# A transformer layer on one NeuronCore: the second FFN product as three products of split operands

## The reference

```python
q = query @ wq + query @ Aq @ Bq * 4.0;  k = query @ wk
v = query @ wv + query @ Av @ Bv * 4.0
q, k = apply_rope(split(q)), apply_rope(split(k))
scores = where(causal, -1e9, einsum('bhqd,bhkd->bhqk', q, k) / 4)
attn_out = (softmax(scores) @ v) @ wo
x = layernorm(x + attn_out)
h = butterfly(x @ W_exp + b_exp, up_weights)
h = gelu(h + up_bias)
y = butterfly(h, down_weights) @ W_con + b_con + down_bias
x = layernorm(x + y)
```

## Time and profile before

| | |
|---|---|
| three runs | 1182.09, 1182.82, 1183.34 us; median 1182.82 us |
| the profiled execution | 1180.9 us, of which its span is 1179.2 us |
| share of the span busy | PE 93%, DVE 71%, ACT 57%, POOL 42% |
| mean granted TensorE clock | 0.962 of full (2.4 GHz); 1.00 from 178 us to 1088 us |
| chain that ended last, by engine | PE 76%, DVE 8%, DMA 8%, issue 3%, ACT 2% |

### The profile page before, as it was taken

One profiled execution on the slowest core, in us unless ns is written; L12 is line 12 of the kernel. 1 busy time (PEld: TensorE's weight loads), 2 busy tenths in 40 slices (PEclk: granted clock), 3 DMA queues, 4 the chain that ended last, 5 costly groups with the idle time before them and its releaser, 6 DMA issues.

```text
span 1179.2 us, 27684 instructions
## 1 busy us (share of the span) xinstructions
PE 1091.7 (93%) x8462; PEld 791.5 (67%) x8462; DVE 840.0 (71%) x1951; ACT 674.4 (57%) x1067; POOL 491.4 (42%) x539
## 2 busy tenths in 40 slices
PE   4677699999999999999999999999999999999976
PEld 3454366767677776767677776767677777766665
DVE  6689867686868678686858678686858778676333
ACT  2277557474656657474656657474656658474601
POOL 5342524435363634435363634435353635433301
PEclk9678799999999999999999999999999999999989
DMA  7773553646465564646465564646465564641201
GB/s 267 162 214 88 167 131 102 185 111 195 93 213 127 182 156 132 174 110 197 95 206 127 182 159 134 169 109 203 93 203 127 181 162 138 166 116 49 74 28 36
DMA packets 94983, 169.90 MB, mean 144 GB/s; under 512 B 14872, under 2 KB 36120, under 8 KB 94944
## 3 DMA queue, kind: packets, MB, share of 16 engines
q1 hardware_dynamic: 93888, 166.53, 51.2%
q10 hardware_dynamic: 832, 1.83, 0.4%
q0 software_dynamic: 224, 1.04, 0.2%
HBM read 92.28 MB, written 77.07 MB: 144 GB/s over the span
## 4 chain that ended last, share of the span: by engine, by line
PE 76%; DVE 8%; DMA 8%; issue 3%; ACT 2%; POOL 1%; SPq 1%; DVEq 0%; POOLq 0%; ACTq 0%
PE ps_m L560 27%; PE ps_m L709 17%; PE ps_m L679 10%; PE ps_m L608 7%; PE ps_t L651 6%; PE ps_m L688 4%; DMA m_scr<-m_row 4%; DVE m_raw L905 2%; PE ps_m L637 2%; DMA q_st<-m_scr 2%; ACT pT L781 1%; DVE gact L991 1%; DVE y L991 1%; PE ps_m L671 1%; PE ps_m L694 1%
## 5 line engine op out<-in xcount | busy, mean ns | idle before, releaser
L781 ACT ACTIVATE pT<-ps_t 128x512 f32<-128x512 f32 x640 | 330.9, 602 | 223.1 <-PE ps_t L651 222.8
L905 DVE TENSOR_REDUCE m_raw<-ps_m 128x1 f32<-128x512 f32 (+2 forms) x768 | 338.6, 505 | 67.8 <-PE ps_m L637 62.3
L1046 POOL TENSOR_SCALAR_AFFINE_SELECT pT<-pT 128x512 f32<-128x512 f32 (+1 forms) x320 | 179.1, 562 | 450.3 <-ACT pT L781 447.4
L709 PE MATMUL ps_m<-w,gact 128*128 128x256 f32 x1024 | 231.6, 382 | 1.1 <-ACT gact L851 1.1
L709 PEld LDWEIGHTS ps_m<-w,gact 128*128 128x128 f32 x1024 | 191.9, 190 | 29.6 <-ACT gact L851 1.5
L608 PE MATMUL ps_m<-k_st,q_st 48*128 48x512 f32 (+3 forms) x1024 | 152.5, 354 | 26.3 <-DMA k_st<-qk_scr 15.1
L679 PE MATMUL ps_m<-pT,v_aug 128*32 128x512 f32 (+3 forms) x2048 | 157.9, 450 | 4.4 <-DVE m_raw L905 3.0
L608 PEld LDWEIGHTS ps_m<-k_st,q_st 48*128 48x128 f32 x1024 | 88.3, 189 | 84.6 <-issue 59.7
L651 PE MATMUL ps_t<-q_st,k_st 50*128 50x512 f32 (+3 forms) x1024 | 129.8, 354 | 12.8 <-DMA q_st<-m_scr 8.6
L952 DVE TENSOR_TENSOR y<-ps_m,y 128x256 f32<-128x256 f32 x64 | 27.2, 425 | 145.9 <-PE ps_m L709 145.9
L679 PEld LDWEIGHTS ps_m<-pT,v_aug 128*32 128x32 f32 x2048 | 58.8, 112 | 90.7 <-issue 78.8
(11 more groups left out here) (106 smaller groups left out, 1601.3 us busy)
## 6 DMA issues: line engine op xcount, KB each, us to landing
qk_scr<-rot_hi SPq DMA_DIRECT2D x64, 512.0 KB, 3.7
q_st<-qk_scr SPq DMA_DIRECT2D x128, 192.0 KB, 4.7
k_st<-qk_scr SPq DMA_DIRECT2D x128, 192.0 KB, 5.0
qk_scr<-rot SPq DMA_DIRECT2D x32, 512.0 KB, 4.0
o_scr<-o_raw SPq DMA_DIRECT2D x64, 256.0 KB, 3.0
r_b<-in_xT SPq DMA_DIRECT2D x17, 512.0 KB, 6.4
o_c<-o_scr SPq DMA_DIRECT2D x32, 256.0 KB
r_b<-r_scr SPq DMA_DIRECT2D x32, 256.0 KB
```

The lines of the kernel that those rows point to most:

```text
L709: mm = pe.matmul(pm[:, 0:D], gact[:, k, n * P:(n + 1) * P], w2[:, k, :], start=(k == 0), stop=(k == NHT - 1))
L781: act.activation(pT[:, g % 2, slot, half * T:(half + 1) * T], ps_t[:, ST_BANK[2 * n + r], :], ACT.Exp, scale=SCALE).then_inc(exp_done, 1)
L905: ins = dve.tensor_reduce(m_raw[:, r, u // 2, qt:qt + 1], scores[:, off:off + (qt + 1) * P], AX.X, ALU.max, negate=True)
L1046: pool.affine_select(out=v, in_=v, compare_op=ALU.is_ge, fill=0.0, base=0, pattern=pattern, channel_multiplier=-1).then_inc(mask_done, 1)
```

## The change

The second FFN product is computed as three products. `w2` becomes `w2_hi` and `w2_lo`. The activation is split by two new steps: `HI` (ACT, two copies of 128x1024 for each half) and `LO` (a subtraction of 128x1024 for each quarter: quarters 0 and 1 on POOL, 2 and 3 on DVE). The pieces of W2 move to phases 3, 3, 4 and 6, those of V to phases 2 and 3. To make room, gact and `g_lo` share one buffer, the upper half of the high part lies in the buffer of x1T, `rot_hi` and `rope_in` are half as large (which adds waits to HIGH and moves a wait of DVE's QK step), the fifth slots of pT are one slot, and set-up tables share a buffer.

```diff
         elif p == 2:
             put("VC", i)
             gemm("QK", i + 1, 3)
             put("QKL", i + 1, 0)
-            gemm("W2", i - 2, 0)
+            if not static or i >= 0:
+                gemm("V", i + 1, 0)
         elif p == 3:
...
-            gemm("W2", i - 2, 1)
+            gemm("V", i + 1, 1)
+            put("LO", i - 2, 2)
+            put("LO", i - 2, 3)
+            gemm("W2", i - 2, 0)
             put("RCP", i - 1, 1)
             put("REC", i - 1, 1)
-            gemm("W2", i - 2, 2)
+            gemm("W2", i - 2, 1)
...
         elif p == 4:
             put("QKL", i + 1, 1)
-            gemm("W2", i - 2, 3)
+            gemm("W2", i - 2, 2)
...
         elif p == 6:
-            if not static or i >= 0:
-                gemm("V", i + 1, 0)
-                gemm("V", i + 1, 1)
+            gemm("W2", i - 2, 3)
             gemm("MT", i, 3)
...
         elif p == 1:
             put("XRES", i - 1, 0)
+            put("HI", i - 2, 1)
...
             put("OUT", i - 2)
+            put("HI", i - 1, 0)
+            put("LO", i - 1, 0)
 
     def last(p):
 
-        if p == 2:
+        if p == 0:
+            put("LO", i - 2, 1)
+        elif p == 2:
             put("ON", i - 1, 0)
...
+        def low_parts(eng, b, j):
+
+            half, part = j // 2, slice(2 * (j % 2), 2 * (j % 2) + 2)
+            g = gact[:, 2 * j:2 * j + 2, :]
+            eng.wait_ge(ghi_done, 4 * b + j + 1)
+            eng.tensor_tensor(g_lo[:, 2 * j:2 * j + 2, :], g, g_hi[half][:, part, :].bitcast(FP32), ALU.subtract)\
+               .then_inc(glo_done[half], 1)
...
                     half = int(kind == "W2B")
-                    pe.wait_ge(gelu_done, 2 * b + half + 1)
-                    for k in range(NHT // 2 * half, NHT // 2 * (half + 1)):
-                        mm = pe.matmul(pm[:, 0:D], gact[:, k, n * P:(n + 1) * P], w2[:, k, :],
-                                       start=(k == 0), stop=(k == NHT - 1))
+                    cols, ks = slice(n * P, (n + 1) * P), range(NHT // 2)
+                    if n == 0:
+                        pe.wait_ge(ghi_done, 4 * b + 2 * half + 2)
+                    for k in ks:
+                        for w in (w2_hi, w2_lo):
+                            pe.matmul(pm[:, 0:D], g_hi[half][:, k, cols], w[:, NHT // 2 * half + k, :],
+                                      start=(half == 0 and k == 0 and w is w2_hi), stop=False)
+                    if n == 0:
+                        pe.wait_ge(glo_done[half], 2 * (b + 1))
+                    for k in ks:
+                        mm = pe.matmul(pm[:, 0:D], g_lo[:, NHT // 2 * half + k, cols],
+                                       w2_hi[:, NHT // 2 * half + k, :],
+                                       start=False, stop=(half == 1 and k == NHT // 2 - 1))
...
+                    if not (isinstance(b, int) and b == 0):
+                        act.wait_ge(qkh_out, 2 * DMA * (2 * b + n))
+                        act.wait_ge(low_done, 2 * b + n)
+                    act.activation(high_of(b, n), rot[:, n, :, :], ACT.Copy).then_inc(high_done, 1)
...
-                    act.activation(w2[:, n, :], pm[:, 0:D], ACT.Copy).then_inc(evac["DM"], 1)
+                    act.activation(w2_hi[:, n, :], pm[:, 0:D], ACT.Copy).then_inc(w2h_done, 1)
...
+                elif kind == "HI":
+
+                    act.wait_ge(gelu_done, 2 * b + n + 1)
+                    wait(act, done["W2"], NT * b)
+                    for j in range(2):
+                        k = NHT // 2 * n + 2 * j
+                        act.activation(g_hi[n][:, 2 * j:2 * j + 2, :], gact[:, k:k + 2, :], ACT.Copy)\
+                           .then_inc(ghi_done, 1)
...
+                elif kind == "DM":
+                    dve.wait_ge(w2h_done, n + 1)
+                    dve.tensor_tensor(w2_lo[:, n, :], pm[:, 0:D], w2_hi[:, n, :].bitcast(FP32),
+                                      ALU.subtract).then_inc(evac["DM"], 1)
+                elif kind == "LO" and n > 1:
+                    low_parts(dve, b, n)
```

More of the change, by code:

```diff
@@ L262, in layer @@
         cs = sb("cs", [P, 2, T])
-        rope_in = sb("rope_in", [P, 4, T])
+        rope_in = sb("rope_in", [P, 2, T])
         rot = sb("rot", [P, 2, 2, T])
-        rot_hi = sb("rot_hi", [P, 2, 2, T], F32R)
+        rot_hi = sb("rot_hi", [P, 2, T], F32R)
         v_new = sb("v_new", [P, NT, D])
@@ L270, in layer @@
         r_b = sb("r_b", [P, 2, T])
-        s_m = sb("s_m", [64, 64])
-        r_m = sb("r_m", [64, 64])
+        small = sb("small", [P, P])
+        s_m, r_m, m_row = small[64:P, 0:64], small[64:P, 64:P], small[0:NM * GH * NT, :]
         x_res = sb("x_res", [P, NT, D])
-        x1T_hi = sb("x1T_hi", [P, KD, T], F32R)
-        x1T_lo = sb("x1T_lo", [P, KD, T], F32R)
-        gact = sb("gact", [P, NHT, T])
+        x1T = sb("x1T", [P, 2, KD, T], F32R)
+        with ExitStack() as before_g_hi0:
+            setup = before_g_hi0.enter_context(nc.sbuf_tensor("setup", [P, P + 32], FP32))
+        g_hi0 = sb("g_hi0", [P, NHT // 2, T], F32R)
+        with ExitStack() as before_g_lo:
+            gact = before_g_lo.enter_context(nc.sbuf_tensor("gact", [P, NHT, T], FP32))
+        g_lo = sb("g_lo", [P, NHT, T], F32R)
         y = sb("y", [P, NT, D])
@@ L351, in layer @@
         rope_done, high_done, low_done = sem("rope_done"), sem("rot_hi_done"), sem("rot_lo_done")
-        qk_out, ones = sem("qk_out"), sem("ones")
+        qkh_out, qkl_out, ones = sem("qk_hi_out"), sem("qk_lo_out"), sem("ones")
         fill = [sem(f"fill{g}") for g in range(NG)]
@@ L359, in layer @@
         lnd = [sem("ln1_done"), sem("ln2_done")]
+        ghi_done, glo_done = sem("g_hi_done"), [sem(f"g_lo{half}_done") for half in range(2)]
+        w2h_done = sem("w2_hi_done")
         x1b_done, gelu_done, out_sent = sem("x1b_done"), sem("gelu_done"), sem("out_sent")
@@ L480, in one @@
                         sp.dma_start(qk_scr[b, n, slot, :, :, :].rearrange("(e i) h t -> (i h) e t", i=8),
[L481 removed]
+                                     high_of(b, n).bitcast(FP32)).then_inc(qkh_out, DMA)
                 elif kind == "QKL":
@@ L484, in one @@
                     sp.dma_start(qk_scr[b, n, 2 - n, :, :, :].rearrange("(e i) h t -> (i h) e t", i=8),
-                                 rot[:, n, :, :]).then_inc(qk_out, DMA)
+                                 rot[:, n, :, :]).then_inc(qkl_out, DMA)
                 elif kind == "FILL":
@@ L489, in one @@
                         sp.wait_ge(ones, 1)
-                    hold(sp, qk_out, QKN * (b + 1))
+                    hold(sp, qkh_out, 4 * DMA * (b + 1))
+                    hold(sp, qkl_out, 2 * DMA * (b + 1))
                     hold(sp, st_done, 2 * (NU * (b - 1) + UG * (n + 1)))
@@ L775, in one @@
                     g, u = n // UG, n % UG
-                    if u == 0:
-                        wait(act, done["PV"], NG * b + g - 1)
+                    if u in (0, GH):
+                        wait(act, done["PV"], NG * b + g - int(u == 0))
                     for r in range(2):
-                        slot, half = (u, r) if u == GH else (2 * (u // 2) + r, u % 2)
+                        slot, half = (2 * GH, r) if u == GH else (GH * (g % 2) + 2 * (u // 2) + r, u % 2)
                         act.wait_ge(st_done, 2 * (NU * b + n) + r + 1)
-                        act.activation(pT[:, g % 2, slot, half * T:(half + 1) * T],
+                        act.activation(pT[:, slot, half * T:(half + 1) * T],
                                        ps_t[:, ST_BANK[2 * n + r], :],
@@ L919, in one @@
                     dve.wait_ge(done["QK"], 4 * b + n + 1)
-                    if n % 2 == 0:
+                    odd = n % 2
+                    if odd:
                         wait(dve, rope_done, 2 * b + n // 2)
-                    a, c = ((0, 0), (1, 1)) if n % 2 == 0 else ((2, 1), (3, 0))
-                    dve.tensor_tensor(rope_in[:, a[0], :], pm, cs[:, a[1], :], ALU.mult)
-                    dve.tensor_tensor(rope_in[:, c[0], :], pm, cs[:, c[1], :], ALU.mult)\
+                        products = rope_in[:, :, :]
+                    else:
+                        if n == 0:
+                            wait(dve, qkl_out, 2 * DMA * b)
+                        products = rot[:, n // 2, :, :]
+                    dve.tensor_tensor(products[:, 0, :], pm, cs[:, odd, :], ALU.mult)
+                    dve.tensor_tensor(products[:, 1, :], pm, cs[:, 1 - odd, :], ALU.mult)\
                        .then_inc(evac["QK"], 1)
@@ L1049, in one @@
                     rot_low(pool, b, n)
+                elif kind == "LO" and n < 2:
+                    low_parts(pool, b, n)
                 elif kind == "XLO":
```

50 lines of the change are left out of this document (24 added, 26 removed).

## The result

The changed kernel takes 1231.05 us (median of four runs, 1229.99 to 1232.28); the kernel before took 1182.45 us beside it. The ratio is 1.0418 (95% interval 1.0393 to 1.0443). The profiled execution takes 1230.9 us, with a span of 1229.1. The sign was forecast; the size was not: 1210 was forecast, 1222 was the top of the range.

The account below looks back on a forecast made before the run. PE's queue, busy 93% of the span, was taken to bound the kernel. 1180.9 + 13 (loop) - 5 (iteration 15) + 3 (iterations 16, 17) + 2 (set-up) + 15 (clock) = 1208.9, stated as 1210 us; range 1163 to 1222, about 0.8.

Parts of the forecast that it names:

- The drain: Last iterations: -5 us for iteration 15 and +3 for iterations 16 and 17 together.
- LO on POOL: Phases 9 and 0: delays the selects by some 4 us, but their reader PV comes later; taken at nothing, at most 1.
- The regular iteration: Iterations 2 to 14: +1.0 us each from pieces, stall and phase 6, with falls of the clock booked on top.
- The price of W2: Each W2 piece on PE: 24 F32R matmuls take 2.94 us against 3.55, 2.44 us less a batch.
- rival 3: Loads bind W2: 65 us more, 1246 and more; chance 0.05, shared with several new waits.
- The stall of phase 2: Phase 2's second S waits for ACT's evacuation of V's piece: a new stall of 3.0 us, bounds 2.8 to 3.2.
- The DMA's wait inside it: Phase 2's second ST waits for the maxima's DMAs, landing about 1.34 us after their last issue: 1.2 us.
- rival 2: Faster: V's evacuation isn't late in phase 2, so no stall; 1170, or 1142 with no wait; chance 0.20.
- VectorE's +0.4 for phase 6: Phase 6: DVE evacuates W2's last piece ahead of m_row's copy; between 0 and 0.43 us, taken at 0.4.
- The balance of pieces and stall: One iteration: the gain of 2.44 us from cheaper W2 pieces is eaten by the 3.0 us stall; +0.6.
- The clock: Behind phase 2's stall the clock falls in 9 of 13 iterations, costing 1.7 us each: +15, bounds 0 and 22.
- The -5 of iteration 15: Iteration 15, without V: pieces -2.44, m_pad's wait covered -2.6, half clock behind it -1.3, LO's lost cover +1.1.

Follow-up runs that it names:

- maxima_first: The changed kernel with the maxima's write and read-back ahead of the raw output and QKH's DMAs in SyncE's phase 1 queue; 1230.3 us, ratio 1.0402.
- filler: The changed kernel with eight extra F32R matmuls of 512 columns in front of phase 2's second ST; 1222.7 us, ratio 1.0344.
- places_only: The kernel before with only V's and W2's pieces at the new places, no HI, LO, split of w2 or shared buffers; 1214.4 us, ratio 1.0259.
- hi_behind_v: The changed kernel with phase 1's HI copies moved behind V's evacuation on ScalarE in phase 2; 1211.2 us, ratio 1.0261.
- four_moves: The changed kernel with HI behind V, maxima ahead of QKH, FILL behind maxima, LO behind phase 9's selects, iteration 16's last W2 piece in phase 4; 1193.9 us.
- moves_loop_lo: four_moves with LO back ahead of phase 9's selects in the loop, and behind them in iteration 15 alone; 1181.0 us, ratio 0.9989.

## Why the prediction was wrong: phase 7 and the drain, behind a regular loop whose errors cancelled

Slower was forecast, by 28 us, and it came by 49.9. Two steps failed. The drain was forecast at -2 us, with "LO on POOL ... taken at nothing, at most 1", and measured +15.7. The wait for the maxima in phase 7 had no term at all, and with the longer falls of the clock it makes most of another 10 us. The regular iteration came out as forecast, 2.2 us longer for 2.15, but its terms did not, so that part is luck.

- **The price of W2** was right: 2.87 us a piece, 2.94 forecast, so rival 3 (loads bind) is out.
- **The stall of phase 2** was right in cause, and nearly in size: 3.0 forecast, and from S to second S it is 3.2 us more. ScalarE's order sets it, as maxima_first shows. The DMA's wait inside it was put at 1.2 us and is 1.97: the prediction took the maxima's arrival from phase 7, 1.34 us after the last issue, and in phase 2, behind QKH's two DMAs, it is 2.2. That costs nothing here, and made rival 2 (V's evacuation not late) worse than it was priced.
- **The iteration without the clock** is 67.0 us in filler, +1.0 over the kernel before, where +0.6 + 0.4 was forecast. VectorE's +0.4 for phase 6 did not come: phases 6 and 7 take what they took. The balance of pieces and stall is +1.0 and not +0.6.
- **The clock** fell behind phase 2 13 times in 13, not 9. But a fall cost 1.2 us (filler) and not 1.7, so the term is 16 us where 15 was booked. The Trainium skill, page "TensorE: Matmul & The Clock Gate", section "HAM oscillation — how this bites in real kernels", which the prediction gave beside its own value, has the slow clock in every pass; the trace agrees for this gap of 2.9 us (13 of 13), and not for one of 1.9 to 2.0 us (4 of 12 in places_only, 8 of 12 in hi_behind_v).
- **Phase 7** had no term. The prediction read 0.56 us in the earlier trace rows as a fixed wait. The write of the maxima ahead of it took 3.6 to 4.7 us in the loop before, and up to 6.0 after. In the changed kernel the clock fell behind two of phase 7's waits, of 2.56 and 1.15 us, and not behind others of 1.09, 1.02 and 1.00. Beyond 7.9 us an iteration, phase 7 took 8.8 us in the twelve iterations, and 1.6 before. With three long falls of the clock (6.8 us each instead of 3.4) this makes most of the 10 us by which the loop lost more than twelve times 2.2. Why the write was slower after, in some iterations, is not shown; that the queue ahead of it is the cause is.
- **The drain** was the step that failed most: -2 forecast, +15.7 measured. "LO on POOL ... taken at nothing, at most 1" rests on PV's late reader; that holds in the loop, where W1 and QK stand between, and not in iteration 16, where nothing does: 3.8 us and a fallen clock. Taking W2's last piece from in front of WO was booked at +1, and opened a wait of 3.2 us more; places_only has that wait too (3.04 us, 1.05 before). The -5 of iteration 15 had the cover of m_pad's wait in phase 6 as its main term. That wait did go. But from its first S to that of phase 5 this batch took 2.3 us more, and here LO on POOL comes in again (DVE, POOL and PE of the changed kernel, phase 0 and 1):

```profile
1090.11 2.30 DVE L960 TENSOR_TENSOR m_pad<-m_raw,m_pad 128x16 fp32r<-128x16 f32 x1
```
```profile
1090.02 2.36 POOL L428 TENSOR_TENSOR g_lo<-gact,g_hi 128x1024 fp32r<-128x1024 f32 x1
```
```profile
1092.55 0.30 PE L695 MATMUL ps_m<-ident,m_pad 128*128 128x128 f32 x1 [1.61 <-DVE m_pad L960]
```

  The subtraction for m_pad takes 2.30 us beside it, where 0.17 to 0.64 is usual, PE waits 1.61 us, and from 1095.0 the clock is 1.2 GHz for 10.2 us.
- **The set-up**: -2.2 against +4.2, inside the scatter of the first column.

Put together: phase 7 and the long falls +10, the drain +18, the regular loop +1 and the set-up -6 make up the 22 us between 28 and 49.9. HIGH's new waits and the shared buffers, which the prediction took at nothing, were not run alone; in phases 0 to 2, where one HIGH stands, ScalarE's 0.15 us of idle time leaves no room for such a wait.

## What to carry to other kernels

When a step is moved in front of a unit, look for every wait of that unit and count how far each has slack, not only the one that comes last: the next one takes its place. A step booked at nothing because of its cover has to be followed through the last iterations, where the cover is missing. Where a wait ends with a DMA, look at what is ahead of it in the queue: one step moved in SyncE's list took away phase 7's waits. An iteration that comes out as forecast proves its terms only when they are measured one by one.

## What the runs showed of the hardware

**Subtractions on GpSimd and VectorE shut each other out.** In the loop of four_moves VectorE's subtraction of 128x16 for m_pad takes 2.31 us, beside POOL's LO; in moves_loop_lo, which differs in LO's place alone, 0.32, and the LO starts behind it. Rows of four_moves, then of moves_loop_lo:

```profile
591.69 2.37 POOL L432 TENSOR_TENSOR g_lo<-gact,g_hi 128x1024 fp32r<-128x1024 f32 x1
591.78 2.31 DVE L964 TENSOR_TENSOR m_pad<-m_raw,m_pad 128x16 fp32r<-128x16 f32 x1
594.02 0.68 DVE L976 TENSOR_TENSOR rot<-ps_m,cs 128x512 f32<-128x512 f32 x1
```
```profile
588.89 0.32 DVE L966 TENSOR_TENSOR m_pad<-m_raw,m_pad 128x16 fp32r<-128x16 f32 x1
...
589.74 2.40 POOL L434 TENSOR_TENSOR g_lo<-gact,g_hi 128x1024 fp32r<-128x1024 f32 x1
```

The small subtraction ends when POOL's does, and PE waits 0.72 us for it (0.95 more for QK behind it). The time lies within its record and not in a wait ahead of it, and no semaphore stands between the two. So the sentence at the start, by which engines wait for one another only through semaphores, doesn't hold for this pair. It works the other way too. Groups of the changed kernel (mean ns of one is the number behind the comma):

```profile
L428 DVE TENSOR_TENSOR g_lo<-gact,x1T 128x1024 fp32r<-128x1024 f32 x32 | 49.7, 1595 | 13.3 <-ACT x1T L894 13.3
L1114 POOL TENSOR_TENSOR o_c<-o_c,r_b 128x512 f32<-128x512 f32 x32 | 55.0, 1717 | 33.7 <-DMA r_b<-r_scr 33.7
```

LO on VectorE costs 1.6 us on average and not the 1.23 of the earlier trace rows, and up to 2.3. POOL's o_c beside it averages 1.72 us, 1.27 before: 14 of the 32 take more than 2.2 us, as the one at 691.19 with 2.26, beside the two LO from 691.06. Reductions from PSUM keep their time (684 ns in both kernels). The Trainium skill, page "SBUF — State Buffer", section "Who interferes with whom", says that a VectorE instruction with two SBUF inputs and a GpSimd one that reads SBUF exclude one another, and that the later one is blocked. The trace agrees: 2.31 us against 0.32.

**A small DMA waits with the large ones ahead of it.** In the changed kernel's twelve iterations it took 1.6 to 1.9 us (once 2.7) from the issue of the 16 KB of maxima to the issue that reads them back where little was queued, and 3.1 to 6.0 us behind 1.3 MB of FILL and x; with the 768 KB of FILL moved behind it, 1.57 us in eleven of twelve.
